# Turning the rows and the gated values of a Hyena block by DMA, with an fp16 forward transform

## The reference

```python
u  = x @ in_proj_w.T + in_proj_b                  # 512 -> 3*512 channels
uc = causal depthwise convolution of u over time, 3 taps, + short_b
x0, x1, v = split(uc, 3)                          # 512 channels each
k  = filter made by a small sine network, times a decay
v  = v * x1                                       # the gated values
v  = irfft(rfft(v, 1024) * rfft(k, 1024))[:512] + v * bias
y  = (v * x0) @ out_proj_w.T + out_proj_b
x  = layernorm(x + y)
g  = silu(x @ Wg.T) * (x @ Wu.T)                  # Wg, Wu, Wd: (integers - 128) * scale
x  = layernorm(x + g @ Wd.T)
```

## Time and profile before

| what | us |
|---|---|
| median of three runs | 990.19 |
| lowest and highest of them | 988.64 and 991.0 |
| profiled execution, its time | 989.24 |
| profiled execution, its span | 987.4 |

### The profile page before, as it was taken

How to read it: one execution, slowest core, us unless ns; L and a number is a source line. 1 busy time by engine, 2 the same in 40 slices (tenths; PEclk the granted TensorE clock), 3 DMA queues, 4 the chain that set the end, 5 groups by cost and what they waited for, 6 DMA issues and landing times.

```text
span 987.4 us, 17405 instructions
## 1 busy us (share of the span) xinstructions
PE 955.4 (97%) x6210; PEld 665.8 (67%) x6210; DVE 762.8 (77%) x1441; ACT 437.2 (44%) x940; POOL 555.6 (56%) x628
## 2 busy tenths in 40 slices
PE   6888999999999999999999999999999999999996
PEld 3345667667676767667676676767677676787774
DVE  6788896887888788787887878787887777686454
ACT  3687543434354343534444343543445344334342
POOL 0268885474747556474765647475564747575210
PEclk9999999999999999999999999999999999999998
DMA  9434400221101211221012211012111110101100
GB/s 300 134 128 131 105 1 1 45 64 22 44 17 27 65 23 43 44 58 27 3 44 44 64 23 44 16 28 65 22 44 23 43 22 10 36 1 44 44 21 22
DMA packets 98953, 47.97 MB, mean 49 GB/s; under 512 B 80048, under 2 KB 84784, under 8 KB 98868
## 3 DMA queue, kind: packets, MB, share of 16 engines
q1 hardware_dynamic: 98370, 46.79, 18.2%
q10 hardware_dynamic: 498, 0.08, 0.0%
HBM read 32.17 MB, written 8.39 MB: 41 GB/s over the span
## 4 chain that ended last, share of the span: by engine, by line
PE 75%; DVE 9%; issue 5%; POOL 4%; ACT 3%; POOLq 0%; DVEq 0%; ACTq 0%
PE gate_up L1316 12%; PE gate_up L1317 12%; PE bank L1159 9%; PE bank L1160 9%; PE bank L1161 9%; PE down L1328 6%; PE down L1329 6%; PE bank L1276 4%; DVE tmp L1068 2%; POOL acc L879 1%; PE spectrum L1159 1%; PE spectrum L1160 1%; PE spectrum L1161 1%; DVE hid_lo L1147 1%; POOL acc L886 1%
## 5 line engine op out<-in xcount | busy, mean ns | idle before, releaser
L885 POOL TENSOR_TENSOR acc<-acc,tmp 128x256 f32<-128x256 f32 x160 | 122.7, 767 | 136.6 <-DVE tmp L1068 124.6
L1068 DVE TENSOR_TENSOR tmp<-spectrum,filt 128x512 f32<-128x512 f32 x256 | 172.7, 681 | 0.5 <-PE spectrum L1161 0.5
L831 ACT ACTIVATE hid<-gate_up,gate_scale 128x256 f32<-128x256 f32 x176 | 82.9, 471 | 195.7 <-PE gate_up L1317 195.6
L1316 PE MATMUL gate_up<-x2T_hi,wg_sb 128*128 128x256 f16 x704 | 163.3, 273 | 0.0
L1317 PE MATMUL gate_up<-x2T_lo,wg_sb 128*128 128x256 f16 x704 | 163.3, 273 | 0.0
L1317 PE MATMUL gate_up<-x2T_lo,wu_sb 128*128 128x256 f16 x704 | 163.3, 273 | 0.0
L1316 PE MATMUL gate_up<-x2T_hi,wu_sb 128*128 128x256 f16 x704 | 163.2, 273 | 0.0
L879 POOL TENSOR_TENSOR acc<-acc,tmp 128x512 f32<-128x512 f32 x96 | 125.3, 1306 | 55.3 <-DVE tmp L1068 55.0
L1159 PE MATMUL bank<-xT_hi,win_hi 128*128 128x512 f16 x360 | 138.1, 384 | 7.2 <-DVE cx L1044 2.3
L838 ACT ACTIVATE hid_hi<-hid 128x256 f16<-128x256 f32 x176 | 73.4, 417 | 145.4 <-DVE hid L1141 145.4
L1160 PE MATMUL bank<-xT_lo,win_hi 128*128 128x512 f16 x360 | 137.8, 383 | 0.0
(11 more groups left out here) (204 smaller groups left out, 1770.8 us busy)
## 6 DMA issues: line engine op xcount, KB each, us to landing
x<-in_x SPq DMA_DIRECT2D x28, 256.0 KB, 2.9
out<-x SPq DMA_DIRECT2D x28, 256.0 KB, 2.1
xstage<-in_x SPq DMA_DIRECT2D x96, 64.0 KB, 2.5
xstage<-in_x SPq DMA_DIRECT2D x12, 256.0 KB, 3.8
more_stages<-in_win SPq DMA_DIRECT2D x7, 256.0 KB, 5.3
x<-in_win SPq DMA_DIRECT2D x5, 256.0 KB, 5.3
acc<-in_decay SPq DMA_DIRECT2D x4, 256.0 KB
x2T_hi<-in_wu SPq DMA_DIRECT2D x4, 256.0 KB, 2.9
```

The source lines that it names most:

```text
L885: G.tensor_tensor(acc[:, i, 0, :], acc[:, i, 0, :], t[:, 1, :], ALU.subtract)
L1068: TT(dst, spectrum[j % 2][:, :, :], k_part, ALU.mult).then_inc(made_done, 1)
L1316: mm(dst, w[:, kb, rows(q)], x2T_hi[:, kb, ts], start=kb == 0, stop=False)
```

## The change

Rows of sequences 1 to 7 (`X_BY_DMA`) are loaded in natural order, in four DMAs of 256 KB for a sequence. `xsplit` splits them in that order into `x_parts` (fp16), and SP turns each part with a `dma_start_transpose`: eight for a sequence, in beats 6 to 9 of odd n, behind a wait for the last `ip` that reads the old `xT`. `xturn` is gone, and so are the four `xt` of sequence 1.

The gated values get a power-of-two scale of their own for each half: `vmax` (one reduction over 1024 columns) and `vscale` (four small operations), both on VectorE at the end of beat 6. `vsplit` then takes `cv` itself, in natural order, in beats 7 and 8: ScalarE writes the high part, VectorE the low part, both fp16, and SP turns each with a `dma_start_transpose`, four in a half. `tv` is gone. `fw` waits for all four, where it waited for the `tv` of its block. `vT` has two buffers.

The forward matrix is scaled by 1024 and split in fp16, so `fw` multiplies fp16 factors. `y` multiplies by the scale that undoes both (`v_out`), with one more operand.

In the first halves `vmax`, `vscale` and `vsplit` of n = 0 and n = 2 are placed by `FILLING`; those of n = 1, and `xsplit` of sequence 1, stand where `beat_steps` puts them.

```diff
+X_BY_DMA = range(1, NSEQ)
...
-    if beat in (7, 8) and ips and n not in (1, 2):
-        steps += [("tv", n, beat - 7)]
-    if beat == 6 and n in (1, 2):
-        steps += [("tv", n, 0), ("tv", n, 1)]
...
     steps += readers([p for p in earlier if p[0] not in ("xt", "x2t")])
+    if beat in (7, 8) and n < HALVES:
+        steps += [("vsplit", n, beat - 7)]
...
-        if beat in (2, 3, 4, 5):
-            steps += [("xturn", following, beat - 2)]
-        if beat in (7, 8, 9, 10):
-            steps += [("xsplit", following, beat - 7)]
+    if n % 2 == 1 and following in X_BY_DMA:
+        if beat in (6, 7, 8, 9):
+            steps += [("xsplit", following, beat - 6)]
+    if beat == 6 and n < HALVES:
+        steps += [("vmax", n), ("vscale", n)]
...
+    ("v1", 0, 1): [("wmax", 7), ("wmax", 8), ("vmax", 0), ("vscale", 0)],
+    ("spec", 0, 1): [("vsplit", 0, 0), ("vsplit", 0, 1)],
+    ("acc", 1, 2, 2, 1): [("vmax", 2), ("vscale", 2), ("vsplit", 2, 0), ("vsplit", 2, 1)],
...
-        vT_hi, vT_lo = (sb(f"vT_{n}", [P, TB, W], F32R) for n in ("hi", "lo"))
+        v_parts = sb("v_parts", [P, 2, 2, L], F16)
+        v_inv, v_scale, v_out = (sb(f"v_{n}", [P, 2], F32) for n in ("inv", "scale", "out"))
+        vT_hi, vT_lo = (sb(f"vT_{n}", [P, 2, TB, W], F16) for n in ("hi", "lo"))
...
+                elif kind == "xsplit" and at[0] in X_BY_DMA:
+                    s, tb = at
+                    sp.wait_ge(bank_ready, use["ip", 2 * s - 1, 1, X0] + 1)
+                    sp.wait_ge(x_hi_done, TB * s + tb + 1)
+                    sp.dma_start_transpose(xT_hi[:, :, rows(tb)], x_parts[:, tb, 0, :]).then_inc(xt_in, 16)
+                    sp.wait_ge(x_lo_done, TB * by_dma_x(s) + tb + 1)
+                    sp.dma_start_transpose(xT_lo[:, :, rows(tb)], x_parts[:, tb, 1, :]).then_inc(xt_in, 16)
...
+                elif kind == "vsplit":
+                    n, c = at
+                    if n > 1:
+                        sp.wait_ge(spectrum_ready, TB * (n - 1))
+                    for part, dst, done in ((0, vT_hi, v_hi_done), (1, vT_lo, v_lo_done)):
+                        sp.wait_ge(done, 2 * n + c + 1)
+                        sp.dma_start_transpose(dst[:, n % 2, :, rows(c)], v_parts[:, c, part, :]).then_inc(vt_in, 16)
...
+                    if s in X_BY_DMA:
+                        STT(out=x_parts[:, tb, 1, :], in0=xstage[:, tb, :], scalar=scale, in1=x_parts[:, tb, 0, :],
...
+                elif kind == "vmax":
+                    n, = at
+                    dve.wait_ge(v1_done, 2 * n + 2)
+                    greatest(v_inv[:, n % 2:n % 2 + 1], flat(cv[:, :, :])).then_inc(v_max, 1)
...
+                    STT(out=y, in0=sums, scalar=v_out[:, n % 2:n % 2 + 1], in1=y, op0=ALU.mult, op1=ALU.mult)\
...
-                        if n // 2 in BY_SQUARES:
-                            pe.wait_ge(x_lo_done, TB * by_squares(n // 2) + TB)
+                        if n // 2 in X_BY_DMA:
+                            pe.wait_ge(xt_in, 32 * TB * (by_dma_x(n // 2) + 1))
...
-                    pe.wait_ge(*read_of(use["tv", n, j // 2]))
+                    pe.wait_ge(vt_in, 64 * (n + 1))
```

More of the change, by code:

```diff
@@ L91, in shared @@
         steps += [("iv", n - 1, INVERSE_OF_BEAT[beat])]
-    if beat in (9, 10) and n % 2 == 1 and n + 1 < HALVES and (n + 1) // 2 not in BY_SQUARES:
-        steps += [("xt", (n + 1) // 2, 2 * (beat - 9) + b) for b in range(2)]
     return steps
-READER = {"ip": "conv", "iv": "y", "op": "ln1", "tv": "vsplit", "xt": "xsplit", "x2t": "x2split", "xs": "xscale"}
+READER = {"ip": "conv", "iv": "y", "op": "ln1", "xt": "xsplit", "x2t": "x2split", "xs": "xscale"}
 def readers(products):
@@ L212, in setup_steps @@
             steps += [("wmax", k) for k in range(7, 13)]
[L213 to L214 removed]
+        elif beat == 7:
+            steps += [("wscale", 2), ("wtaps", 2), ("scales", )]
         steps += [("stage", k) for k in STAGE_OF_BEAT.get(beat, ())]
[L216 to L217 removed]
     if (n, beat) in SPEC_OF_BEAT:
@@ L255 @@
     ("ip", 2, 1, 2): [("op", 0, 1)],
-    ("acc", 1, 2, 3, 1): [("conv", 2, 1, 2), ("ln1", 0, 1), ("stat", LN1, 0, 1), ("var", LN1, 0), ("vsplit", 2, 0),
-        ("vsplit", 2, 1), ("norm", LN1, 0)],
+    ("acc", 1, 2, 3, 1): [("conv", 2, 1, 2), ("ln1", 0, 1), ("stat", LN1, 0, 1), ("var", LN1, 0), ("norm", LN1, 0)],
     ("x2t", 0, 0): [("mul", 1, 3, 3, 0), ("acc", 1, 3, 3, 0), ("mul", 1, 3, 3, 1), ("acc", 1, 3, 3, 1)],
@@ L341, in build @@
         steps = program()
-        use = count(steps, "xt", "ip", "tv", "iv", "op", "x2t")
+        use = count(steps, "xt", "ip", "iv", "op", "x2t")
         convs = count(steps, "conv")
@@ L1242, in _ @@
                     mm(sums_of_set(which), ones[:, :], of_set(which, w_stat), start=True, stop=True).then_inc(sums_done, 1)
-                elif kind == "tv":
-                    n, jp = at
-                    k = use["tv", n, jp]
-                    dst = free_bank(k)
-                    pe.wait_ge(v1_done, 2 * n + 2)
-                    for j in range(2):
-                        for c in range(2):
-                            last = nc.tensor.transpose(dst[:, (2 * j + c) * P:(2 * j + c + 1) * P], cv[:, c, rows(2 * jp + j)],
-                                                       ident[:, :])
-                    last.then_inc(bank_ready, 1)
                 elif kind == "fw":
@@ L1263, in _ @@
                     for r in range(2):
-                        last = three(spectrum[k % 2][:, r, :], [(fwd_hi[:, rows(r)], fwd_lo[:, rows(r)], vT_hi[:, j, :],
-                                                                 vT_lo[:, j, :])])
+                        last = three(spectrum[k % 2][:, r, :], [(fwd_hi[:, rows(r)], fwd_lo[:, rows(r)], vT_hi[:, n % 2, j, :],
+                                                                 vT_lo[:, n % 2, j, :])])
                     last.then_inc(spectrum_ready, 1)
```

121 lines of the change are left out of this document (56 added, 65 removed).

## The result

The changed kernel took 1005.5 us, median of four runs (1003.98 to 1008.53); the kernel before, on the same chip, 990.3 (988.64 to 991.0). The ratio is 1.016, with a 95% interval of 1.013 to 1.019: slower, by some 15 us. The profiled execution took 1004.15 us, with a span of 1002.4.

A forecast was written before the change was run, and what follows sets the result against it. TensorE was taken to bound the kernel from n = 3 on, with VectorE coming last in odd halves: 989.24 + 11.6 (n = 1) + 1.7 (clock) + 2.8 (n = 2) + 0.5 (n = 0) - 6.5 (steady halves) = 999.3 us, range 985 to 1012.

The forecast's parts named there:

- lower clock behind it: After TensorE's pause ahead of the first `ip` of n = 2: time at 1.2 GHz costs 1.7 us, bounds 0 and 3.4.
- n = 2: New VectorE work ahead of `ln1`, `stat` and `var`, 3.4 us, delays norm and transposes by 2.8, bounds 0 and 3.4.
- SP's queue in n = 1: Transposes at 1.29 us each fall behind; first `ip` of n = 2 at 100.6 against 89.00, 11.6 us later.
- Rival A: On SP, a transpose holds the queue like a plain load, 0.43 us: `ip` 4.3 late, 992.0 us in all; chance 0.13.
- TensorE's pause: Ahead of the first `ip` of n = 2: TensorE idle for some 10 us, with a lower clock behind it.
- The 3.4 us gap covers: Steady halves: VectorE's idle 2.60 us ahead of `ln1` and 0.80 ahead of `conv` take 2.65 us of additions, 0.7 to spare.
- Rival C: Steady halves: VectorE's idle gap doesn't cover the additions, 2 us a half paid, 1031.8 us at worst; chance 0.12.
- Odd halves: Steady odd n: VectorE's stretch from `conv` to `hid_lo` grows 0.2, `dn` waits about 1 us, each half gains 0.1.
- Even halves: Steady even n: VectorE's run loses one `vT_lo`, `hid_lo` comes 0.6 earlier, each half gains 0.85 us.
- TensorE's relief: Steady halves: two `tv` gone, 0.87 us, and four faster `fw`, 0.26, together 1.13 us a half.
- Rival D: Steady halves: `fw` isn't faster in fp16, costing 3.4 us of relief at most, 1002.7 us; counted with the forecast, no own chance.
- Rival B: VectorE's additions are hidden and TensorE leads everywhere: steady halves gain 14.7 us, 986.0 us in all; chance 0.17.

The follow-up runs named there:

- the copies: Changed kernel with the twelve transposing DMAs of n = 1 (eight of x, four of v) as plain copies of the same bytes: 1001.99 us, ratio 1.0123.
- the run with TensorE at work: Changed kernel with 100 extra matmuls ahead of the first `fw` of n = 1 and 15 ahead of the first `ip` of n = 2: 1002.62 us.
- the two kernels with the moves: VectorE's steady-half scale, x splits and one `xmax` moved; v by TensorE, 984.09 us, or v by DMA with n = 0 to 2 as before, 973.58 us.
- the x part alone: Changed kernel's handling of x for sequences 2 to 7 only; sequence 1 and all of v as in the kernel before: 987.15 us, ratio 0.9977.

## Why the prediction was right, and where its terms were wrong

It said 999 us, 985 to 1012, and slower with a chance of 0.69. The forecast's mechanism is what happened: a queue that falls behind in n = 1, a small gain afterwards. But the profiled execution is 5 us above the forecast's value, the median 6.5. The terms stand like this in the profiled execution (the last column from the balance; `ip` from its own start):

| term | predicted | measured |
|---|---|---|
| n = 0 | +0.5 | +1.3 |
| n = 1, start of the first `ip` of n = 2 | +11.6 | +11.0 |
| lower clock behind it | +1.7 | +2.7 |
| n = 2 | +2.8 | +4.0 |
| n = 3 to the end | -6.5 | -4.0 |
| sum | +10.1 | +15.0 |

All terms but one erred to the same side. So the range held by its width, and not because errors cancelled. With n = 0 as it ran in the other profiles (the last section) the sum would be 2 us larger still.

- **SP's queue in n = 1: right.** The last issue was put at 98.1 and the `ip` at 100.6; they are at 98.69 and 101.33, and 1.3 us of the latter came from n = 0. That one transpose holds the queue for 1.25 us, from the rows of `x2dma`, was the number that carried the forecast. Rival A, a transpose priced like a plain load, is refuted twice: by the rows, and by the copies, whose 0.6 to 0.7 us gave 7.4 back. The Trainium skill ("Advanced Engine Details and Errata", X-Bar Transpose (TRN2)) says that transposing DMAs are as fast as regular ones. For the landing these runs agree (2.4 to 2.8 us against 2.4 to 2.9); for the time on the queue they don't (1.25 against 0.65), and here the queue is what counts.
- **TensorE's pause: right in kind, too small.** I expected an idle of 10 us ahead of the `ip`. There are two, 12.59 us ahead of `fw` and 3.21 ahead of `ip`; I had not followed `fw`, which waits for v as well. The clock's price I read from a window of before that lost 1.7 us. The 12 `ip` alone lost 12 times 0.21, 2.5, and the run with TensorE at work gave 2.4 back.
- **n = 2: the term was too small.** The step took 1.2, 0.7 and twice 0.75 us, less a margin of 0.6. In the rows it is 4.4 from `vmax` to `ln1`: the splits took 0.95 each, and VectorE waited 0.74 for ScalarE's high part, which the step left out. That v's landing holds `fw` for 2.73 us I had not seen at all; the run with v behind the norm shows that it would have cost more.
- **The 3.4 us gap covers: right.** It is filled to 0.16 and 0.72, as the sum of 2.65 with 0.7 to spare said, and taking `vmax` away changes nothing. Rival C falls.
- **Odd halves: right in kind.** From `conv` to `hid_lo` VectorE takes 12.41 us in n = 9 (522.15 to 534.56) where it took 12.22: the 0.2 that was put. `dn` waits 1.09 us, where I said about 1. The six halves gain 2.0 us in sum, not 0.6, since two of them (n = 3 and n = 7) gain 0.8 and 0.9; the others go from 0.2 lost to 0.4 gained, in two lengths that the last section takes up. The 57.5 us that I named as their length were too few: from n = 5 on they take 57.8 to 58.4.
- **Even halves: wrong, the step that failed.** VectorE's run ahead of `hid_lo`, so the prediction, "loses one `vT_lo` (0.6 between starts) to an earlier beat with idle time". It does not. Both `v_parts` stand behind the `conv`, at 466.74 and 470.84, in the stretch that ends with `hid_lo` at 476.96; nothing left it. `hid_lo` starts 45.30 us into the half, where it was 45.49: 0.2 earlier, not 0.6. So `dn` waits 0.47, and n = 6, 8 and 12 gain 0.36 to 0.38, not 0.85. Besides, n = 4 loses 0.97 with its wait for `x2T`, which the prediction had put at nothing, and n = 10 nothing to speak of (0.03 lost). Only n = 14 and n = 15 (counted to the end of the span) gain what was put, 0.95 and 0.99. The seven gain 2.05 in sum, where 5.95 was put; the odd halves give 1.4 of the difference back, and the sum missed 2.5.
- **TensorE's relief: 1.0 us a half, where 1.13 was put.** It shows where nothing waits: 57.14 to 56.12 in the two kernels with the moves, and 0.95 in n = 14 of the changed kernel. Two `tv` at 0.43 are 0.86 of it, which leaves some 0.15, not 0.26. Rival D is not the reason: six matmuls of `fw` take 0.66 us from the first start to the next `dn` (557.16 in the changed kernel), 0.109 each as put, where they took 0.80 or more. Where the other 0.1 stays is not shown.
- **Rival B (TensorE leads everywhere)** was not this kernel, but it was near: with VectorE's list rearranged and n = 0 to 2 as before, the balance falls by 14.6 us from n = 3 to n = 15, and its price for the steady halves was 14.7. But some 3 us of it come from the moves alone, with v on TensorE too.
- The earlier trace rows carry the labels n = 7 and n = 8; counted by the `conv` of v they are n = 9 and n = 10. No step depends on it.

**Open:** where the x part alone takes its 2.2 us. An odd half is 0.38 shorter and an even one 0.14 longer than before, and on TensorE's list the difference comes in steps of 0.03 to 0.11 us, not at one wait; no run took that apart. Also open is what sets the waits for `x2T`. The v part alone, with x by squares, was not tried.

## What to carry to other kernels

A transfer that moves work off the bound engine is paid for where its queue has no time to hide it: price one issue on the queue, multiply by the transfers of the stage that has the least cover, and leave that stage as it was if another way exists there. Relief of the bound engine counts only up to the engine that comes last behind it; find that engine's stretch, with its start and its end, and check of every moved instruction whether it has really left that stretch. When a change loses in one stage and gains in another, run each stage with the other's version: here the two halves of the answer were 19 us lost and 13.5 us not collected.
